# A decoder layer with sorted experts: the order of the shared expert's pieces within nine blocks

## The reference, cut to what matters

```python
logits = x @ gate_w.T
scores = softmax(logits)
topk_w, topk_i = top_k(scores, 2)                      # 2 of 8 experts
topk_w = topk_w / topk_w.sum(-1) * 2.5
g = silu(einsum('td,edf->etf', x, w_gate)) * einsum('td,edf->etf', x, w_up)     # F = 176
y = einsum('te,etd->td', combine, einsum('etf,efd->etd', g, w_down))
shared = (silu(x @ sw_gate) * (x @ sw_up)) @ sw_down   # FS = 352
out = layernorm(x + y + shared)
```

## The kernel before, in words

| p | PE, shared piece | ACT and DVE, beside the blocks' own work |
|---|---|---|
| 0, 1, 2 | gate and up | `all_gate`, `all_product` |
| 3, 4, 5, 6 | down quarters 0 to 3 | |
| 7 | none | `all_hi`, `all_lo` of the next group, then `add_shared` |
| 8 | none | |

## Time and profile before

### The profile page before, as it was taken

The page is one execution under the profiler, slowest core; times in us unless marked ns, Lnnn a source line. Parts: engine busy times, 40 slices in busy tenths (PEclk is TensorE's granted clock), DMA queues, the critical chain, the costliest instruction groups (busy, mean ns, idle before and its releaser), DMA issues. The chain is left out here.

```text
span 2050.2 us, 47315 instructions
## 1 busy us (share of the span) xinstructions
PE 1952.0 (95%) x15971; PEld 1687.8 (82%) x15971; DVE 1493.5 (73%) x3900; ACT 1278.6 (62%) x3929; POOL 1299.2 (63%) x1467
## 2 busy tenths in 40 slices
PE   7999969999999999999999999999999989899995
PEld 4565559999999999999999998999999877787773
DVE  5999946777777777777777778777777755455674
ACT  4777646666666666666666666666666654444564
POOL 4888746666666666666666666666666554344665
PEclk9999979999999999999999999999999989999998
DMA  4200000000000000000000001000000012222454
GB/s 132 75 19 19 19 21 7 14 17 17 16 16 19 17 17 16 16 17 19 17 16 16 15 22 35 17 16 14 22 15 12 10 49 70 85 70 73 123 152 128
DMA packets 103985, 75.27 MB, mean 37 GB/s; under 512 B 10999, under 2 KB 97639, under 8 KB 103623
## 3 DMA queue, kind: packets, MB, share of 16 engines
q1 hardware_dynamic: 94806, 54.20, 9.6%
q0 software_dynamic: 8640, 17.97, 2.5%
q10 hardware_dynamic: 304, 0.07, 0.0%
HBM read 39.64 MB, written 32.57 MB: 35 GB/s over the span
## 5 line engine op out<-in xcount | busy, mean ns | idle before, releaser
L1036 POOL TENSOR_TENSOR x_prob<-x_prob,x_inv 128x496 f32<-128x496 f32 x512 | 519.7, 1015 | 462.7 <-DVE x_inv L1189 460.0
L1116 ACT ACTIVATE x_prob<-x_ps_S,x_nmax 128x248 f32<-128x248 f32 x1024 | 471.1, 468 | 223.6 <-DVE x_nmax L1183 222.0
L1183 DVE TENSOR_REDUCE x_nmax<-x_ps_S 128x2 f32<-128x496 f32 x512 | 343.0, 670 | 107.0 <-PE x_ps_S L859 100.2
L1131 ACT COPY x_probT<-x_ps_T 124x512 f32<-124x512 f32 x512 | 300.2, 587 | 168.5 <-PE x_ps_T L1373 164.1
L857 PE MATMUL x_ps_S<-x_kT_lo,x_G_hi 128*128 128x248 f32 x1024 | 327.8, 320 | 0.0
L1373 PE MATMUL x_ps_T<-ident,x_prob 128*124 128x128 f32 x2048 | 318.5, 278 | 8.6 <-POOL x_prob L1036 7.6
L1373 PEld LDWEIGHTS x_ps_T<-ident,x_prob 128*124 128x124 f32 x2048 | 233.1, 140 | 74.3 <-POOL x_prob L1036 31.0
L859 PE MATMUL x_ps_S<-x_kT_hi,x_G_hi 128*128 128x248 f32 x1024 | 284.6, 278 | 0.0
L858 PE MATMUL x_ps_S<-x_kT_hi,x_G_lo 128*128 128x248 f32 x1024 | 284.5, 278 | 0.0
L1343 PE MATMUL x_ps_O<-x_probT,x_V 124*64 124x128 f32 x4096 | 251.9, 276 | 0.7 <-ACT x_probT L1131 0.7
L1614 POOL DMA_INDIRECT sorted_results<-e_y,w_wkv x142 | 144.3, 1016 | 155.9 <-DVE e_y L1747 148.9
(11 more groups left out here) (248 smaller groups left out, 4427.1 us busy)
## 6 DMA issues: line engine op xcount, KB each, us to landing
w_wkv<-sorted_rows SPq DMA_DIRECT2D x142, 66.0 KB
e_back<-sorted_results SPq DMA_DIRECT2D x32, 256.0 KB, 3.6
latents<-lin_nlat SPq DMA_DIRECT2D x32, 128.0 KB, 1.8
turned_rows<-w_rows SPq DMA_DIRECT2D x32, 128.0 KB, 1.7
w_wq<-turned_rows SPq DMA_DIRECT2D x32, 128.0 KB
out_dram<-e_result SPq DMA_DIRECT2D x16, 256.0 KB, 2.4
x_nk<-latents SPq DMA_DIRECT2D x32, 124.0 KB
x_nk<-in_ctx SPq DMA_DIRECT2D x32, 120.0 KB, 2.2
```

The lines of the kernel that those rows point to most:

```text
L1036: nc.gpsimd.tensor_tensor(prob[:, k], prob[:, k], inv[:, k].unsqueeze(2).broadcast_to([P, 2, K]), ALU.mult).then_inc(prob_ready, 1)
L1116: nc.scalar.activation(prob[:, k, h, :], ps_S[:, n % BANKS, h * K:(h + 1) * K], ACT.Exp, bias=nmax[:, k, h:h + 1], accum_out=total[:, k, h ...
L1131: nc.scalar.copy(probT[0:KT, s % (2 * GANG)], ps_T[0:KT, s % 2, :]).then_inc(probT_ready, 1)
L1183: nc.vector.tensor_reduce(nmax[:, k, :], ps_S[:, n % BANKS, 0:2 * K].rearrange("p (h k) -> p h k", h=2), AX, ALU.max, negate=True).then_in ...
```

## The change

`PIECES` becomes 7. In the groups of nine steps position 3 carries no piece any more, and the four down quarters move to positions 4 to 7; position 8 carries none, as before. `add_shared` follows the last quarter and is so issued at position 8. `load_all` is issued two steps earlier (t = 9g - 7), `all_hi` two steps earlier (position 5 of the group before) and `all_lo` one step earlier (position 6). The last two groups keep their seven steps. The amount of computation is the same.

| p | PE, shared piece | ACT and DVE, beside the blocks' own work |
|---|---|---|
| 0, 1, 2 | gate and up | `all_gate`, `all_product` |
| 3 | none | |
| 4, 5, 6, 7 | down quarters 0 to 3 | `all_hi` at 5, `all_lo` at 6 |
| 8 | none | `add_shared` |

```diff
-    PIECES = 8
+    PIECES = NS + GROUP
...
             if t >= LATE_FROM:
-                g, k = divmod(t - LATE_FROM, PIECES - 1)
+                g, k = divmod(t - LATE_FROM, PIECES)
                 g += GROUPS - LATE
             else:
                 g, k = divmod(t - SHARED_FROM, EVERY)
-                if g >= GROUPS - LATE or k >= PIECES:
+                if g >= GROUPS - LATE or k in (NS, EVERY - 1):
                     return None, None
+                k -= k > NS
             return (g, k) if 0 <= g < GROUPS else (None, None)
...
-                g = prepared_at(t + 13)
+                g = prepared_at(t + 15)
                 if g is not None and g > 1:
                     load_all(g)
...
-                g = prepared_at(t + 2)
+                g = prepared_at(t + 4)
                 if g is not None:
                     all_hi(g)
...
-                g = prepared_at(t + 2)
+                g = prepared_at(t + 3)
                 if g is not None:
                     all_lo(g)
                 g, k = shared_at(t - 1)
-                if g is not None and k == PIECES - 2:
+                if g is not None and k == PIECES - 1:
                     add_shared(g)
...
-                elif k < NS + GROUP:
+                else:
```

## The result

The changed kernel takes 2043.21 us in the median of its runs (2038.91 to 2048.83), the kernel before beside it 2059.06 (2056.97 to 2060.3): a ratio of 0.9926 with an interval of 0.9911 to 0.9941, 15.9 us less. Forecast was 2033.4, with a range from 2027 to 2043. So the direction was right and the gain was 15.9 us instead of 25.3; the median lies just above the upper end of the range. The profiled execution took 2038.91 us (span 2037.2) against 2051.95 (span 2050.2), 13.0 less. The two profiles are not quite alike: the one of the kernel before is 5.0 under the fastest of that kernel's six timed runs, the one of the changed kernel is the fastest of its six. I take the length of the steps apart first.

The account below looks back on a forecast made before the run. PE, busy 95% of the span, bounds the kernel, so its waits count. Groups save 22.3 us (1.59 each in 14), loads 3.9, small debts cost 0.9: -25.3 from 2058.7 gives 2033.4 us, range 2027 to 2043.

Parts of the forecast that it names:

- The pair `all_lo` and `add_shared`: Position 8: without these two DVE operations ahead, the light step falls from 2.30 to 1.28, saving 1.02 us a group.
- down quarter 0 no longer waits for `all_product`: Position 4: `all_hidden` is long there, so the quarter's step falls from 2.83 to 1.93, saving 0.90 us a group.
- the forecast 2.3: Step 45: PE waits 2.3 us (1.6 to 2.5) for row loads behind the closing stores; this part saves 3.9 us.
- the return path and the other engines take everything back: Whole stage: DVE or POOL sets the pace and waits only move, giving about 2058 us; chance 0.03.
- the clock falls in every group: All 14 groups: the thinned PE work drops the clock, costing 2.2 us each, 2064 us; chance 0.03.
- I cost both at nothing: Positions 5 and 6: `all_hi` and `all_lo` are covered by down quarters; without cover each costs up to 0.6 us a group.
- 1.59 forecast: Position 3, the free step: `lo` behind `all_product` makes it 1.59 us, the wait falling from 0.90 to 0.31.
- 0 to 0.6 lost, I take 0.3: Ramp: `all_hi(0)` and `all_lo(0)` move to steps 4 and 5, where `all_lo` gets ahead of DVE's routing; 0.3 us lost.
- the 2 us that the prediction itself named as a sign of being wrong: Position 3: the prediction is wrong if the free step is longer than 2 us.
- the bounds of -1 to +1.5: Return path: `add_back` meeting light steps and `all_lo` costs 0.3 us, from -1 to +1.5.
- four meetings each: Return path: `add_back` meets light steps four times at positions 6 and 7 before, four times at 2 and 7 now.
- the clock falls once, after the wait: After step 45's wait for rows: a slow stretch costs 2.2 us more, giving 2035.6 us; chance 0.2.

Follow-up runs that it names:

- e6: The changed kernel with closing stores spread one per step and the last `all_product` issued behind `lo` of the next step: 2023.91 us, ratio 0.9862.
- e2: The changed kernel with the stores of `close_regions` issued one in a step from step 30, not all nine there: 2027.83 us (0.9886), repeated 2029.58 (0.9883).
- e3: The changed order of pieces with `load_all`, `all_hi` and `all_lo` at the times of the kernel before: 2040.95 us, ratio 0.9949.
- the repeats: The changed kernel measured three more times, unchanged: 2032.53, 2032.44 and 2032.76 us, ratios 0.9913, 0.9904 and 0.9907 against the kernel before.
- e1: The changed kernel with `all_hi` and `all_lo` one step earlier, at positions 4 and 5: 2032.55 us, ratio 0.9906.
- e12: e6, but PE reads no expert's number at position 8 and two at position 0: 2031.85 us, ratio 0.9867.
- r3_after: Third repeat of the unchanged changed kernel, the "second" profile of the study's tables: 2032.76 us, ratio 0.9907, span 2028.8.
- e5: The changed kernel with the changes of e1 and e2 together: 2028.55 us, ratio 0.9881.
- e13: e12 with the register read of position 3 also moved to position 0, three reads there: 2039.12 us, ratio 0.9898.
- the two profiles of the table: The changed kernel's first profiled execution, span 2037.2 us, and that of r3_after, span 2028.8, against the kernel before, 2050.2.
- e7: e6 with `all_hi` and `all_lo` one step earlier, except group 0's, which go back to step 6: 2023.26 us, ratio 0.9862.
- e11: e7 with PE's read of the next expert's number moved behind the down products: 2029.12 us, ratio 0.9885.
- e4: The order of the kernel before with the changed kernel's times of `load_all`, `all_hi` and `all_lo`: 2043.93 us, ratio 0.9963.
- e9: The changed kernel with the register read of the expert's number made twice in each step, at its old place: 2094.37 us, a single run.
- e10: e6 with PE's read of the next expert's number moved behind the down products: 2029.86 us, ratio 0.9889.
- e8: The changed kernel with PE's read of the next expert's number moved behind the down products: 2034.51 us, ratio 0.9905.
- r1_after: First repeat of the unchanged changed kernel: 2032.53 us, ratio 0.9913.
- after: The changed kernel's first measurement and profile: median 2043.21 us, ratio 0.9926, profiled execution 2038.91.
- r2_after: Second repeat of the unchanged changed kernel: 2032.44 us, ratio 0.9904.
- the second profile above: The profile of r3_after: span 2028.8 us against 2050.2 for the kernel before.

## Why the prediction was right in direction and too large

**Right.** The pair `all_lo` and `add_shared` is gone from ahead of the light step; down quarter 0 no longer waits for `all_product` (position 4 is 2.07 with the slow restart, and 1.93 without it in e6); positions 0 to 7 of a group sum to 18.02 where the forecast's add up to 17.96. The wait for `load_all` in step 43 went and a wait of 2.33 for rows appeared where it was forecast; e2 shows its cause, and e3, which keeps the old wait, shows that the earlier load is what removes it. That 2.33 meets the forecast 2.3 so well is in part luck: the repeats have 3.16, 1.77 and 1.45, and only two of the four lie in the range of 1.6 to 2.5. That the return path and the other engines take everything back (2058) or that the clock falls in every group (2064) is refuted: all repeats are 19 us faster, and from 1813.4 to 1910.9, groups 5 to 9 of the changed kernel, the granted clock is 1.00.

**Wrong: `all_hi` and `all_lo` "I cost both at nothing".** This is the step of the prediction that failed. The argument looked at the chain over `hi` and `lo`, which indeed has room, and not at what PE itself must do before `turn_hidden`: wait for that `lo` and read a register. With `all_lo` ahead of it, `lo` ends 0.64 before the `turn_rows` of position 8 and not 1.03, and the step takes 1.47. e1 gives `lo` its 1.03 back, e12 leaves it at 0.64 and takes the read away, and each alone gives 1.28: both are shown to be needed for the 1.47. That it is the lead of PE's sequencer over PE which they share is argued, no row shows it. The term is 0.19 a group in groups 5 to 9, 2.7 us if all 14 groups have it. Summed over the 14, position 8 takes 22.70 in r3_after and 20.29 in e1, 2.4 less. The times of e1 and e5 show none of it, as said above.

**Right size, half the reason: position 3.** 1.65 was measured, 1.59 forecast, and the waiting for `lo` is there. But e6 took it away and 1.65 stayed; e13 shows the register read to be a second limit of the same size. That the number came out right although one of two limits was overlooked is luck. What holds PE's sequencer back at position 3 is not shown: there `lo` has ended 1.38 before `turn_rows`, more than the 1.03 that is enough at position 8. What `lo` behind `all_product` costs alone is the restart at position 4, 0.14.

**Too small: the ramp (steps 0 to 7).** "0 to 0.6 lost, I take 0.3" measured 1.5 and 1.3 in the two profiles of the table; over all four of the changed kernel and both of before the means are 20.0 and 19.3, so 0.7, and the kernels that leave `all_hi(0)` and `all_lo(0)` where they were (e3, e7, e11) have 18.9 to 19.2, while e4, with the old order and the new times, has 19.91. So it is the earlier preparation of group 0 that costs. These steps vary by 0.8 from one execution to the next, and the term was too small by 0.4 to 1.2.

**Too small: the return path.** The free step was listed as meeting `add_back` in step 110 (issued in 109) and priced, with all such meetings, at 0.3. In r3_after it takes 2.70 there, and 2.38 and 2.16 in steps 119 and 128, longer than the 2 us that the prediction itself named as a sign of being wrong. DVE and PE in step 110:

```profile
1917.42 0.68 DVE L1763 TENSOR_TENSOR e_all_hidden<-e_all_silu,e_ps_up 96x512 f32<-96x512 f32 x1
1918.02 0.68 DVE L1778 TENSOR_TENSOR e_hsum<-e_back,X 128x512 f32<-128x512 f32 x1
...
1919.14 0.28 DVE L1732 TENSOR_TENSOR e_xT_lo<-e_ps_x,e_xT_hi 128x128 fp32r<-128x128 f32 x1
```

```profile
1919.56 0.30 PE L1826 MATMUL e_ps_x<-ident,w_wkv 128*128 128x128 f32 x1 [0.94 <-DVE e_xT_lo L1732]
```

Group 11 takes 22.11 instead of 22.27, so it gains next to nothing, and steps 98 to 133 together gained 4.9 and not 6.1: a debt of 1.4 against the 0.3 taken, just inside the bounds of -1 to +1.5 and position 8's share included. e6, in which `all_product` is out of the way of this `lo`, has 1.95 and 1.90 in steps 110 and 119.

**Missing: steps 134 to 140.** The sum had no term for them and the kernels with the new order pay 0.6 to 1.4 there (e9 more; e10 and e11 nothing, which is not explained, since e8, with the read at the same place, pays 0.9). `add_shared(13)` now is issued in step 133, the same step as an `add_back`. In r3_after DVE has both and two statistics ahead of `lo`, and PE waits for it, step 134 taking 2.55 instead of 1.90:

```profile
1972.51 0.68 DVE L1771 TENSOR_TENSOR X<-X,e_ps_s 128x512 f32<-128x512 f32 x1
1973.11 0.69 DVE L1778 TENSOR_TENSOR e_hsum<-e_back,X 128x512 f32<-128x512 f32 x1
1973.83 0.49 DVE L1782 BATCH_NORM_STATS2 e_stat<-e_hsum 128x6 f32<-128x128 f32 x2
1974.23 0.27 DVE L1732 TENSOR_TENSOR e_xT_lo<-e_ps_x,e_xT_hi 128x128 fp32r<-128x128 f32 x1
```

```profile
1974.65 0.30 PE L1826 MATMUL e_ps_x<-ident,w_wkv 128*128 128x128 f32 x1 [0.77 <-DVE e_xT_lo L1732]
```

I had listed the meetings of `add_back` with light steps ("four meetings each") and not the meeting of `add_back` with `add_shared`, which moved from step 105 (group 10) to step 133 (group 13).

**The clock.** The rival "the clock falls once, after the wait" had a chance of 0.2. It came in two of the seven profiles that have this wait (r1_after and e1, 3.16 and 2.67 idle), and not in after, r2_after, r3_after, e4 and e8 (2.33, 1.77, 1.45, 1.29 and 1.25). The Trainium skill, "TensorE: Matmul & The Clock Gate", section "HAM oscillation — how this bites in real kernels", describes such falls behind waits for DMA; here the two longest of the seven gaps agree with it, and after the five shorter ones no fall came. It cost 1.5 and 1.3 us in step 45 (4.40 and 4.12 instead of 2.85), not 2.2.

**The sum.** The repeats gain 19.1 to 19.8 us in time and, in the second profile above, 21.4 in the span. Of the 3.9 between that and the forecast, the table has 3.1 in the fourteen groups, of which position 8 is 2.7 by the estimate above, 1.0 in the ramp and 1.0 in the tail, and an earlier start of the stage 1.1 the other way. The first measurement, 15.9, is 3 to 4 us lower still; its profile has the stall of 4.8 us in steps 11 and 12. Whether its other runs had it too can't be seen, since only profiled executions show it. That the stall makes the difference to the repeats is not shown: the execution that has it is the fastest of its six, and e12, whose profile has a stall as well, gained 28.0 us where e6, without one, gained 28.6.

**Open.** What ACT and DVE stood still for in steps 11 and 12. They stand idle for 2 to 4 us in three profiles (after, e12 and e13), between 1700 and 1710 us of the span, marked "remote" or "issue", or put to an instruction that had ended long before. These are the three profiles of kernels with the new order that were taken where the kernel before needed 2059 to 2060 us in the median; none taken where it needed 2052 to 2053 has the stall. The profile of the kernel before has none either, but with 2051.95 us it belongs to the second kind by its time, so no run tells whether the stall comes with the new order or with the place. The page of the changed kernel lists 135 and 99 transfers of instructions; whether such a transfer was late can't be read from it, and no run tried anything on it.

## What to carry to other kernels

A light step on TensorE has two costs, the matmuls' and the sequencer's: when a step gets as short as about 1.3 us, count the register reads and how long before the step the wait ahead of them ends, not only the busy rows. When an operation is moved, list every place where it meets other work on its queue over the whole loop, its first and its last group too, since here the regular middle was nearly right and the ends were not. And profile the same kernel more than once before a gain of one per cent is taken apart: here the first profile had 4.8 us in it that the next three did not.

## What the runs showed of the hardware that was not expected

A second register read in each step costs 0.44 us in the mean, 0.7 and 0.9 in the light steps (1.65 to 2.35 and 1.47 to 2.36), nothing at position 0, and stands in no row: the profile shows only a later matmul with "issue". Reading a third number in one step cost 0.5. The Trainium skill, "Runtime: NRT & Kernel Launch", section "Instruction fetch mechanics", gives about 200 ns a register for the instruction `TENSOR_LOAD`, and calls loads round trips. The numbers here lie in SBUF, and the runs show no single read by itself, only these differences.

Two gaps of nearly one length at the same place had different effects: 2.33 us left the clock at 1.00, 2.67 us was followed by 0.59 (a mean over 1777 to 1780 us in e1, which was at 1.2 GHz for most of it and then at 2.4).
